# The delta-rule recurrence of a four-layer kernel: output projection inside its steps, key sum as a column of ones, contiguous PSUM writes with a reordering copy

## What is computed

```python
def step(carry, seg):
    mem, z = carry
    qq, kk, vv = seg
    sigma_q = elu(qq) + 1.0
    scores = where(causal_mask, einsum('bhsk,bhtk->bhst', qq, kk) / scale, -inf)
    att_dot = softmax(scores) @ vv
    att_mem = sigma_q @ mem / (sigma_q @ z)
    sigma_k = elu(kk) + 1.0
    delta = vv - sigma_k @ mem / (sigma_k @ z)
    mem_new = mem + einsum('bhsk,bhsv->bhkv', sigma_k, delta)
    z_new = z + sigma_k.sum(tokens)
    att = beta * att_mem + (1.0 - beta) * att_dot
    out = att.reshape(Bsz, SEG, H * DV) @ Wo
```

## Time and profile before

| | before |
|---|---|
| runs, us | 2040.75, 2037.61, 2035.45 |
| median, us | 2037.61 |
| profiled execution: its own time, us | 2039.76 |
| its span, us | 2038.0 |
| instructions | 27403 |
| mean granted TensorE clock | 0.933 |
| TensorE matmul busy | 1781.8 us, 87% |
| TensorE weight load busy | 1440.3 us, 71% |
| VectorE busy | 1081.2 us, 53% |
| ScalarE busy | 872.8 us, 43% |

### The profile page before, as it was taken

The page is one execution under the profiler, slowest core; times in us unless marked ns, Lnnn a source line. Parts: engine busy times, 40 slices in busy tenths (PEclk is TensorE's granted clock), DMA queues, the critical chain, the costliest instruction groups (busy, mean ns, idle before and its releaser), DMA issues. The chain is left out here.

```text
span 2038.0 us, 27403 instructions
## 1 busy us (share of the span) xinstructions
PE 1781.8 (87%) x9315; PEld 1440.3 (71%) x9315; DVE 1081.2 (53%) x2163; ACT 872.8 (43%) x1690; POOL 243.9 (12%) x236
## 2 busy tenths in 40 slices
PE   5988786987689999999787969969999899999898
PEld 4676645775568888888644858857888788878755
DVE  2266435233545555555656345566665676567466
ACT  3466424333243343333675334354443444344344
POOL 2010002212022222222101212220000000000000
PEclk8999886998789999999898979979999999999989
DMA  2000030110034334332100023210000000000100
GB/s 103 6 14 11 0 132 0 39 31 0 18 101 114 108 110 118 115 108 82 52 0 15 32 57 114 82 58 17 17 16 0 15 15 15 0 15 0 41 0 21
DMA packets 47075, 91.50 MB, mean 45 GB/s; under 512 B 7697, under 2 KB 24081, under 8 KB 46810
## 3 DMA queue, kind: packets, MB, share of 16 engines
q1 hardware_dynamic: 47026, 90.89, 14.9%
HBM read 89.52 MB, written 1.35 MB: 45 GB/s over the span
## 5 line engine op out<-in xcount | busy, mean ns | idle before, releaser
L438 PE MATMUL bank<-l1m_src_hi,l1m_w_hi 128*128 128x512 f32 x384 | 150.2, 391 | 7.4 <-DVE l1m_src_lo L507 7.4
L438 PE MATMUL bank<-l1m_src_lo,l1m_w_hi 128*128 128x512 f32 x384 | 150.0, 391 | 0.0
L438 PE MATMUL bank<-l1m_src_hi,l1m_w_lo 128*128 128x512 f32 x384 | 149.9, 390 | 0.0
L410 POOL TENSOR_TENSOR l1m_w_lo<-l1m_w,l1m_w_hi 128x512 fp32r<-128x512 f32 x96 | 104.8, 1110 | 325.9 <-ACT l1m_w_hi L475 325.9
L514 DVE TENSOR_TENSOR l1m_a<-l1m_s,bank 128x512 f32<-128x512 f32 x96 | 66.0, 687 | 116.3 <-ACT l1m_s L487 116.3
L491 ACT ACTIVATE l1m_a_hi<-l1m_a 128x512 fp32r<-128x512 f32 x96 | 60.7, 633 | 146.5 <-DVE l1m_a L520 146.5
L2091 PE MATMUL bank<-l_mem,l_sg 128*128 128x129 f32 x480 | 95.0, 316 | 30.2 <-ACT l_mem L2221 15.4
L2091 PEld LDWEIGHTS bank<-l_mem,l_sg 128*128 128x128 f32 x480 | 67.9, 195 | 55.8 <-ACT l_mem L2221 44.4
L528 DVE TENSOR_TENSOR l1m_a_lo<-l1m_a,l1m_a_hi 128x512 fp32r<-128x512 f32 x96 | 66.4, 692 | 70.8 <-ACT l1m_a_hi L491 70.8
L2370 DVE RECIPROCAL l_inv<-bank 128x1 f32<-128x1 f32 x240 | 38.9, 162 | 115.4 <-PE bank L2091 115.4
L2221 ACT ACTIVATE l_mem<-bank 128x128 f32<-128x128 f32 x240 | 59.8, 276 | 90.5 <-PE bank L2080 90.0
(11 more groups left out here) (537 smaller groups left out, 4561.9 us busy)
## 6 DMA issues: line engine op xcount, KB each, us to landing
l1m_w<-in_l1f_win SPq DMA_DIRECT2D x48, 256.0 KB, 2.9
l1m_wr<-l1f_token_weights SPq DMA_DIRECT2D x32, 384.0 KB, 3.5
l1m_wr<-l1f_token_weights SPq DMA_DIRECT2D x32, 256.0 KB, 3.9
l_w<-in_l_w SPq DMA_DIRECT2D x9, 768.0 KB, 4.4
wmod<-in_wmod SPq DMA_DIRECT2D x4, 1536.0 KB, 10.1
l1m_w<-in_l1f_wout SPq DMA_DIRECT2D x48, 128.0 KB, 3.1
l1m_wr<-l1f_token_weights SPq DMA_DIRECT2D x32, 128.0 KB, 3.2
l2e_wr<-l2f_token_weights SPq DMA_DIRECT2D x16, 256.0 KB, 3.9
```

Source lines behind the costliest of these rows:

```text
L410: pool.tensor_tensor(w_lo[:, half, part], w[:, half, part], w_hi[:, half, part].bitcast(F32), ALU.subtract).then_inc(split_, 1)
L438: last = pe.matmul(k.bank[:, 2 * c + part, :], wq[:, half, at:at + P], xq[:, b, chunk(c)], start=(b == 0 and q == 0), stop=(b == DB - 1 an ...
```

## The change

TensorE's `project_out` is cut in seven parts of 5, 5, 5, 5, 4, 4 and 4 matmuls, issued in steps 1 to 7 of the recurrence of the next pair; the other pieces move to steps 8 to 15, in larger units. VectorE's `key_sums` goes: a 129th column of `dr` holds -1 (and `nkt` holds minus the keys), so `write_memory` accumulates z in the memory's own PSUM bank, which `first_divisor` starts with a matmul of ones. Memory copies carry 129 columns. `local_attention` and `turn_reads` write PSUM in token order, `dot_scale` and `add_reads` work on a new tile `out` in token order, and ScalarE's new `place_out` (two instructions of 128x1024 per pair) reorders it into `att`. The openings of all three engines are reordered, banks are dealt anew (values in banks 0 to 3, the projection in bank 3), ScalarE copies both halves of the first head's transposed keys, the parts of the next weights are made in steps 3, 5 (high) and 7, 9 (low), and `add_projection` moves to step 8.

```diff
-    MEM, READ, Y, SCORES = 4, 6, 4, (5, 2)
-    V_BANKS = (2, 0)
+    MEM, READ, Y, SCORES = 4, 6, 3, (5, 0)
+    V_BANKS = (0, 2)
+    Y_AT = (0, 5, 10, 15, 20, 24, 28, 32)
...
-        z = sb("z", [P, 2, HP, PAD + NS + 1])
-        mem = sb("mem", [P, HP, NS, P + 2])
-        dr = sb("dr", [P, HP, NS, P])
+        first_z = sb("first_z", [P, P + 2])
+        mem = sb("mem", [P, HP, 2, P + 2])
+        dr = sb("dr", [P, HP, NS, P + 2])
...
+        out = sb("out", [P, HP, T])
         att = k.h[:].rearrange("p a (j c) -> p a j c", j=H)
+        att_by_segment = k.h[:].rearrange("p a (j g r) -> p a g j r", j=H, r=R)
...
+                step.link(pool, pool.memset(first_z[:], 0.0))
+                step.link(pool, pool.memset(first_z[:, P:W1], 1.0 / (P * P)))
+                step.link(pool, pool.memset(dr[:, :, :, P:P + 2], -1.0))
...
-                def project_out(turn):
-
...
+                def project_out(turn, part):
+
+                    if part == 0:
+                        pe.wait_ge(s["att_ready"], turn * HP)
+                    for mj in range(Y_AT[part], Y_AT[part + 1]):
+                        m, j = mj // H, mj % H
+                        last = pe.matmul(k.bank[:, Y, m * P:(m + 1) * P], wo[:, j, tile(m)], att[:, :, j, :],
+                                         start=(j == 0), stop=(j == H - 1))
+                    if part == len(Y_AT) - 2:
+                        last.then_inc(s["y_ready"], 1)
...
+                            if not first and t == 0:
+                                pe.wait_ge(s["reads_added"], i * 4 - 2)
+                            if not first and t == 4:
+                                pe.wait_ge(s["reads_added"], i * 4)
...
+                    def first_divisor(a):
+
+                        pe.matmul(k.bank[:, MEM + a, 0:W1], k.ones[:], first_z[:, 0:W1], start=True, stop=False,
+                                  skip_group_check=True)
...
-                        pe.matmul(k.bank[:, MEM + a, 0:P], nkt[:, a, n // 2, n % 2, :], dr[:, a, n, :], start=(n == 0),
+                        pe.matmul(k.bank[:, MEM + a, 0:W1], nkt[:, a, n // 2, n % 2, :], dr[:, a, n, 0:W1], start=False,
...
-                                last = pe.matmul(segment_rows(2 + c, 2 * (t % 4) + o), v[:, t, a, o, :],
+                                at = (t % 4) * P + o * S
+                                last = pe.matmul(k.bank[:, 2 + c, at:at + S], v[:, t, a, o, :],
...
-                            last = pe.matmul(segment_rows(2 * a + c, n % 8), dr[:, a, n, :], turn[:, half], start=True,
-                                             stop=True)
+                            at = (n % 8) * S
+                            last = pe.matmul(k.bank[:, 2 * c + a, at:at + S], dr[:, a, n, 0:P], turn[:, HALF[1 - n % 2]],
+                                             start=True, stop=True)
...
                     projections(0)
-                    if not first:
-                        pe.wait_ge(s["qk_copied"], i * 8 + 1)
-                        project_out(i)
+                    values()
                     scores(0)
-                    values()
                     keys_by_token(0)
                     projections(1)
                     keys_by_token(1)
                     scores(1)
                     for a in range(HP):
+                        first_divisor(a)
+                    for a in range(HP):
                         write_memory(0, a)
                     for n in range(1, NS):
                         for a in range(HP):
                             read_memory(n, a)
-                        if n in (1, 2):
-                            turn_probs(0, n - 1)
-                        if 3 <= n <= 6:
-                            local_attention(0, (n - 3) // 2, (n - 3) % 2)
-                        if n in (7, 8):
-                            turn_probs(1, n - 7)
-                        if 9 <= n <= 12:
-                            local_attention(1, (n - 9) // 2, (n - 9) % 2)
-                        if n in (13, 14):
-                            turn_reads(n - 13, 0, range(0, 8))
+                        if n <= 7 and not first:
+                            project_out(i, n - 1)
+                        if n in (8, 10):
+                            for c in range(NCH):
+                                turn_probs((n - 8) // 2, c)
+                        if n in (9, 11):
+                            local_attention(0, (n - 9) // 2)
+                        if n in (12, 13):
+                            local_attention(1, n - 12)
+                        if n in (14, 15):
+                            turn_reads(n - 14, 0, range(0, 8))
...
+                def place_out(turn):
+
+                    act.wait_ge(s["reads_added"], turn * 4)
+                    for a in range(HP):
+                        act.activation(att_by_segment[:, a], out[:, a].rearrange("p (g j r) -> p g j r", j=H, r=R),
+                                       ACT.Identity).then_inc(s["att_ready"], 1)
...
+                        if a == 0:
+                            act.activation(nkt[ODD, a, :, 1, :], k.bank[ODD, at:at + 2, :].rearrange(
+                                "p n (t q) -> p (n t) q", q=P), ACT.Identity, scale=-1.0
+                                ).then_inc(s["kt_odd_copied"], 1)
...
                     for j in range(4):
                         queries_keys(j)
                     place_keys(0)
+                    if not first:
+                        place_out(i)
                     values_copy(0)
+                    values_copy(1)
                     exponential(0)
-                    values_copy(1)
                     keys_copy(0)
                     for j in range(4, 8):
                         queries_keys(j)
+                    keys_copy(1)
+                    act.activation(dr[:, :, 0, 0:P], v[:, 0, :, 0, :], ACT.Identity, scale=-1.0
+                                   ).then_inc(s["first_ready"], 1)
                     place_keys(1)
-                    keys_copy(1)
-                    act.activation(dr[:, :, 0, :], v[:, 0, :, 0, :], ACT.Identity, scale=-1.0
-                                   ).then_inc(s["first_ready"], 1)
                     for n in range(NS - 1):
                         for a in range(HP):
                             mem_copy(n, a)
-                        if n in (0, 1):
-                            probs_copy(0, n)
                         if n == 2:
                             exponential(1)
-                        if n in (3, 5):
-                            dot_scale(0, (n - 3) // 2)
-                        if n in (6, 7):
-                            probs_copy(1, n - 6)
-                        if n in (8, 10) and not final:
-                            high_part(i + 1, (n - 8) // 2)
+                        if n in (3, 5) and not final:
+                            high_part(i + 1, (n - 3) // 2)
+                        if n in (8, 10):
+                            for c in range(NCH):
+                                probs_copy((n - 8) // 2, c)
                         if n in (9, 11):
-                            dot_scale(1, (n - 9) // 2)
+                            dot_scale(0, (n - 9) // 2)
+                        if n in (12, 13):
+                            dot_scale(1, n - 12)
...
+                place_out(PAIRS)
...
-                    def key_sums(a):
-
...
                     for j in range(4):
                         sigma(j)
-                    key_sums(0)
                     if not first:
-                        dve.wait_ge(s["att_ready"], i * HP)
+                        dve.wait_ge(s["reads_added"], i * 4)
                     step.link(dve, dve.tensor_copy(bt[:, 0, :], beta[:, bass.ds(i * HP, HP)]))
                     step.link(dve, dve.tensor_scalar(bt[:, 1, :], bt[:, 0, :], -1.0, 1.0, ALU.mult, ALU.add))
-                    if not first:
-                        add_projection(i)
+                    values_copy(0)
+                    values_copy(1)
                     read_scores(0)
                     largest(0)
                     shift(0)
-                    values_copy(0)
+                    for j in range(4, 6):
+                        sigma(j)
                     total(0)
                     normalize(0, 0)
                     normalize(0, 1).then_inc(s["probs_ready"], 1)
-                    values_copy(1)
-                    keys_copy(0)
-                    for j in range(4, 8):
+                    for j in range(6, 8):
                         sigma(j)
                     keys_copy(1)
-                    key_sums(1)
                     read_scores(1)
                     for n in range(1, NS):
                         for a in range(HP):
...
                             normalize(1, 0)
                         if n == 6:
                             normalize(1, 1).then_inc(s["probs_ready"], 1)
-                        if n in (10, 12) and not final:
```

(54 more changed lines are left out.)

55 lines of the change are left out of this document (15 added, 40 removed).

## The result

The changed kernel takes 2052.41 us (median, 2051.33 to 2053.70), the kernel before 2037.61 (2035.45 to 2043.63) beside it: ratio 1.0066, interval 1.0047 to 1.0085. It is slower, by more than the 0.3% that a measurement can tell.

A forecast was written before the change was run, and what follows sets the result against it. TensorE's own stream was taken to bound each pair. Undisturbed pairs 0, clock +4, first pair +3 and end +2.3 made +9 on the profiled 2039.76, with the median 2.15 below: 2047 us, range 2022 to 2059.

The forecast's parts named there:

- TensorE's stream sets the pair, the steps are full: Whole pair: TensorE busy 64.1 of 69.3 us; moving the 7.23 us projection into equally full steps saves nothing alone.
- ScalarE's delays go, 1.9 per pair: Recurrence steps: reads no longer wait for ScalarE's dot_scale and probability copies, some 0.3 in six steps, 1.9 us per pair.
- New opening: Pair's opening: second read of step 1 at 26.7, 2.2 us later, behind VectorE's second-head key copy; pair 69.2 against 69.21.
- The late key copy doesn't bind: Opening: VectorE's second-head key copy ends before 23.7, not 25.9; pairs save 2.2 us, 2025 us; chance 0.15.
- Steps 8 to 14: Later recurrence steps: 8 and 10 take 2.4 us each, 9 and 11 to 13 3.02 (9 adds 0.2), 14 3.10.
- PSUM runs: Attention and transpose writes: contiguous PSUM gains taken as zero; rival says runs were the price, 1999 us, chance 0.05.
- Clock in pairs 2 to 8, +4: Recurrence starts: clock falls in every pair at 1.1 us each, against four falls of 0.9 before; +4 us.
- First pair, +3: First pair, no projection: steps 1 to 7 near 2.0 us, later steps, end and opening longer; +3, bounds 0 and 5.
- End, +2.3: After the last pair: nothing covers place_out, 1.9 to 2.8 us, and the projection follows a longer idle; +2.3 us.
- Clock costs no more than now: Opening wait: the clock fall comes wholly inside the longer wait; +5 instead of +9, 2042 to 2043 us; chance 0.18.
- Opening slower still: Opening and steps: low-clock projection passes at 1.8 per pair (+5) and 0.6 more wait each (+4); 2056 us; chance 0.20.
- the others came: Remaining signs: steps 1 to 4 at 2.5 us, no ScalarE wait, over 2 us at second write_memory, 64-column passes 0.104 to 0.109.

The follow-up runs named there:

- key sum as a column: Kernel before, with the key sum as a 129th column of ones, VectorE's key_sums removed and a first_divisor matmul per head; 2022.62 us, ratio 0.9913.
- copies one step later: Kernel before with the column of ones for key sums, plus ScalarE's probability copies and dot_scale one step later; 2015.71 us, ratio 0.9876.
- best order: Changed kernel, first head's softmax out of the opening: exponential(0) after segment 0's memory copies, total(0) and normalize(0) in steps 3 to 5; 2008.16 us, ratio 0.9841.
- the run with runs of four: Changed kernel with local_attention and turn_reads writing PSUM again in runs of four floats 32 apart; 2052.28 us, ratio 1.0062.
- with the clock held up: Changed kernel with ten unused 128-column matmuls between write_memory(0, 0) and write_memory(0, 1) of every pair; 2045.34 us, ratio 1.0035.
- filled steps: Changed kernel with 32 unused matmuls like the projection's in steps 1 to 7 of the first pair; 2050.96 us, ratio 1.0054.
- VectorE's half alone: Changed kernel with only total(0) and normalize(0) taken out of VectorE's opening, ScalarE's queue unchanged; 2018.66 us, ratio 0.9901.
- ScalarE's half: Changed kernel with only ScalarE's exponential(0) moved behind the key copies, between queries_keys(5) and (6), VectorE's order unchanged; 2037.97 us, ratio 0.9994.

## Why the prediction was right

The forecast, slower, with 2047 in a range of 2022 to 2059, holds; the size was short by 5 us. That range takes in faster kernels as well as slower ones, so the sharper tests are the forecast's own 2042 to 2054 and the terms below. Two of these are off in opposite directions: the clock in pairs 2 to 8 came out 2 us cheaper and the first pair 6 us dearer. The undisturbed pair, laid out from the kernels between the two:

| from | to | us per pair | what it is |
|---|---|---|---|
| before, 69.21 | key sum as a column, 68.07 | -1.14 | wait for the key sums |
| | copies one step later, 66.80 | -1.27 | ScalarE's delays |
| | best order, 65.25 | -1.55 | projection in the steps, attention behind it, values first |
| | the change, 69.29 | +4.04 | first softmax in the opening |

- **TensorE's stream sets the pair, the steps are full.** Right. From the copies one step later to the best order, the projection's move into the steps and all else of the new order are worth 1.55 us per pair together, not the 7.23 that leave the opening; 0.36 of it is the opening's wait for `l_dr` (2.9 in eight pairs with the copies one step later, 0 in the best order).
- **ScalarE's delays go, 1.9 per pair.** The waits do; taking them out of the old order gave 1.27, because four steps of a pair carry the delay and not six. The prediction's own difference of 4.7 says so too: 7.23 less 1.14 leaves 1.4 for them, and the other 0.5 went under "roundings".
- **New opening.** Right within half a microsecond: 1.4 predicted at `keys_by_token(1)`, 1.51 measured; 2.5 at `write_memory(0, 1)`, 2.62 measured; VectorE's key copy at 25.9, measured 26.3; the pair at 69.2, measured 69.29. The last agrees better than its parts do: in pair 3 step 2 starts 29.4 into the pair, not 28.9, and what follows takes 39.9, not 40.3. The reasons are right, too, by the runs with VectorE's and ScalarE's part alone. What the prediction didn't ask is how cheaply the order is mended.
- **The late key copy doesn't bind** (rival, 2025): false; the wait is in all eight pairs, and without it pairs are 4.04 shorter, not 2.2.
- **Steps 8 to 14.** Right: two chunk steps are 3.09 apart, 3.02 predicted.
- **PSUM runs.** Zero was right; the rival at 1999 is refuted by the run with runs of four.
- **Clock in pairs 2 to 8, +4.** The first term that was mis-sized, too high. A pair with a fall costs 1.39 more, above the 1.1 taken; but the fall comes in four of seven pairs, as before, not in all. Net +2.0, and with 0.08 per pair the +2.4 of the table.
- **First pair, +3.** The step that failed. Its working forms (empty steps at about 2.0, opening 2.2 longer) give, with the clock held up, 69.14 against 66.24: +2.9, nearly the forecast. (The 66.24 have a fall in them that the term left out, PEclk 0.58 from 1380 to 1384; by the 0.9 that a fall cost before, the forms alone are worth +3.8, my estimate.) The missing 6.05 us are clock: I costed it only in the pairs with projection in their steps, and there a fall costs 1.39; in the empty steps it lasted 23.5 us.
- **End, +2.3.** Measured +2.6: ScalarE's `place_out` of 2.0 us with nothing over it, and the projection 9.59 for 9.04. ScalarE's row, then TensorE's:

```profile
1918.05 2.00 ACT L2205 ACTIVATE h_modulated<-l_out 128x1024 f32<-128x1024 f32 x2 [7.11 <-DVE l_out L2390]
```

```profile
1920.11 9.59 PE L2021 MATMUL bank<-h_modulated,l_wo 128*128 128x128 f32 x64 [3.31 <-ACT h_modulated L2205]
```

- **Clock costs no more than now** (rival, 2042 to 2043): false, through the first pair; in pairs 2 to 8 alone it was half right. **Opening slower still** (2056): false, 69.29.

The terms inside the stage sum to 8.95 + 2.4 + 2.6 = 13.9 against 9.3 predicted; before and behind it the profiled execution is 2.3 us shorter, with the same code.

Of the signs that the prediction named, "PEclk 0.5 at the start of every recurrence" failed in pairs 3, 5 and 7, the first pair lies outside the "69 to 71 us", and the profile names no releaser where `l_nkt` was expected; the others came.

What stays open: why the clock falls in every second pair of the change and not in each, with the same wait in all; how much idle time it takes, since before, two waits of 0.99 and 0.85 brought falls and here one of 1.5 alone did not; and which part of the 1.55 us belongs to the projection's place and which to the other moves of the new order.

## What to carry to other kernels

When two heads' work stands in one in-order queue, ask of each piece who needs it first: the softmax is wanted in step 8 or so, the second head's key copy at once, and standing the wrong way round they cost 44 us, more than all the rest of the change gains. Idle time of the matmul engine is not only its own length: count what runs thinly behind it, because there the low clock lasts. Separate a change of many parts by kernels with one part each; here the key sum alone was worth 0.9%, and the whole lost 0.7%.

## What the runs showed of the chip

- An idle stretch of TensorE of 2.6 us ahead of thin work was followed by 23.5 us at granted clock 0.50 (the 1.2 GHz level); with filled steps it was back at 1.00 some 6.5 us after the matmuls resumed. The same thin steps without the idle stretch ran at 1.00 throughout.
- With an unchanged wait in every pair the clock fell in pairs 2, 4, 6 and 8 and stayed at 1.00 in 3, 5 and 7. With VectorE's half alone (a wait of 1.5 at the transposes, 0.2 at the write) there was no fall, with ScalarE's half (2.2 at the write) there still were some. The length of the longest wait doesn't settle it: in the kernel before, waits of about 1.0 and 0.85 close together were followed by falls in pairs 1, 3, 6, 7 and 8, and the key-sum kernel, with 0.35 in place of both, had none.
- Keeping TensorE busy with matmuls that nobody reads shortened the eight pairs by 11.6 us.
